# A decoder layer on one core: the mask's score bound moved into self-attention's tail, weight splits moved to a step's begin, first queries ahead of the values

## What is computed

```
x = layernorm(x + self_attention(x))          # 32 heads of 16, causal, biases on q, k, v and out
x = layernorm(x + cross_attention(x, ctx))    # 32 query heads, 8 key/value heads of 128, rotary angles, mask
x = layernorm(x + experts(x))                 # 16 experts of 256, 4 of them per token, and a shared one

# cross-attention, the part that the change touches:
scores = einsum('bhgqd,bhkd->bhgqk', qg, k) / sqrt(128)
masked = where(mask.astype(bool), scores, -1e9)
w = softmax(masked, axis=-1)
```

## Time and profile before

| | |
|---|---|
| median of 3 runs | 1770.8 us (1770.31 to 1776.01) |
| the profiled execution's own time | 1773.97 us |
| its span, first to last instruction | 1772.2 us |
| granted TensorE clock, mean | 0.982 of full |
| PE / DVE / ACT / POOL busy | 96 / 72 / 52 / 54 % |
| self-attention | 0 to 303 us |
| cross-attention | 303 to about 1300 us |
| experts | behind that |

### The profile page before, as it was taken

The page is one execution under the profiler, slowest core; times in us unless marked ns, Lnnn a source line. Parts: engine busy times, 40 slices in busy tenths (PEclk is TensorE's granted clock), DMA queues, the critical chain, the costliest instruction groups (busy, mean ns, idle before and its releaser), DMA issues. The chain is left out here.

```text
span 1772.2 us, 39039 instructions
## 1 busy us (share of the span) xinstructions
PE 1695.6 (96%) x15461; PEld 968.1 (55%) x15461; DVE 1267.5 (72%) x2048; ACT 919.0 (52%) x1518; POOL 964.8 (54%) x875
## 2 busy tenths in 40 slices
PE   6899998699999999999999999999889999999997
PEld 4666665365555555555555555555555555455553
DVE  5777776678888888888888888888786444344445
ACT  5776764555546564646464555455742333333334
POOL 5556672745645454646464646464743555455545
PEclk9999999899999999999999999999988999999999
DMA  4522312311312222214131222121166778887658
GB/s 147 146 65 47 85 48 36 117 37 58 110 62 83 83 68 89 97 42 149 37 108 61 72 72 96 37 104 40 61 226 198 153 151 222 221 208 153 115 100 300
DMA packets 88897, 190.68 MB, mean 108 GB/s; under 512 B 14800, under 2 KB 33744, under 8 KB 86672
## 3 DMA queue, kind: packets, MB, share of 16 engines
q1 hardware_dynamic: 65232, 130.72, 22.1%
q0 software_dynamic: 22912, 57.32, 15.8%
q10 hardware_dynamic: 576, 0.14, 0.0%
HBM read 124.95 MB, written 63.21 MB: 106 GB/s over the span
## 5 line engine op out<-in xcount | busy, mean ns | idle before, releaser
L1112 POOL TENSOR_TENSOR xa_sc<-xa_sc,xa_rs 128x1024 f32<-128x1024 f32 x32 | 60.9, 1903 | 374.4 <-DVE xa_rs L1360 374.4
L1099 POOL TENSOR_TENSOR xa_xs<-xa_xs,sn 128x512 f32<-128x512 f32 x160 | 234.1, 1463 | 45.7 <-ACT xa_xs L1153 45.7
L288 PE MATMUL bank<-xhl,front_h 128*128 128x512 f16 x640 | 245.4, 383 | 10.9 <-DVE front_l L648 9.7
L289 PE MATMUL bank<-xhl,front_h 128*128 128x512 f16 x640 | 245.2, 383 | 0.0
L290 PE MATMUL bank<-xhl,front_l 128*128 128x512 f16 x640 | 245.0, 383 | 0.0
L1104 POOL TENSOR_TENSOR xa_rr<-xa_x,xa_xs 128x512 f32<-128x512 f32 x160 | 232.9, 1456 | 12.7 <-DVE xa_x L1260 0.2
L2006 POOL DMA_INDIRECT scratch_y<-raw_front,moe_to x79 | 125.3, 1586 | 149.1 <-DVE mo_zl L2060 126.8
L288 PE MATMUL bank<-out_h,xa_oh 128*128 128x512 f16 x512 | 194.1, 379 | 10.3 <-DVE xa_ol L1242 6.7
L290 PE MATMUL bank<-out_h,xa_ol 128*128 128x512 f16 x512 | 194.0, 379 | 0.0
L289 PE MATMUL bank<-out_l,xa_oh 128*128 128x512 f16 x512 | 194.0, 379 | 0.0
L1152 ACT ACTIVATE xa_xs<-bank 64x512 f32<-64x512 f32 x160 | 95.1, 595 | 140.7 <-PE bank L290 126.5
(11 more groups left out here) (318 smaller groups left out, 4665.5 us busy)
## 6 DMA issues: line engine op xcount, KB each, us to landing
xa_rawc<-in_ew SPq DMA_DIRECT2D x32, 768.0 KB, 5.5
moe_ring<-scratch_w SPq DMA_DIRECT2D x16, 1536.0 KB
scratch_w<-xa_chunk_h SPq DMA_DIRECT2D x32, 384.0 KB, 2.3
scratch_w<-xa_chunk_l SPq DMA_DIRECT2D x32, 384.0 KB, 3.3
raw_front<-in_xwq SPq DMA_DIRECT2D x8, 1024.0 KB, 7.8
raw_out<-in_xwo SPq DMA_DIRECT2D x8, 1024.0 KB, 5.3
scratch_y<-acc SPq DMA_DIRECT2D x6, 1024.0 KB, 5.8
acc<-in_x POOLq DMA_DIRECT2D x4, 1024.0 KB, 7.7
```

The source lines that it names most:

```text
L288: pe.matmul(out_ap, ah, bh, start=start and m == 0, stop=False)
L289: pe.matmul(out_ap, ah, bl, start=False, stop=False)
L1099: PO.mark(pool.tensor_tensor(xr, xr, sn[:, :].rearrange("p (a s) -> p a s", a=1) .to_broadcast([P, QT // S, S]), ALU.mult), f"sm{r}", st)
L1112: PO.mark(pool.tensor_tensor(s4, s4, rs[:, :, :].rearrange("p h (t a) -> p (h t) a", a=1) .to_broadcast([P, 16, S]), ALU.mult), "nm", st)
```

## The change

1. `bound` becomes a buffer that lives through both attentions. Its bytes (128 partitions by 2048 f32) serve self-attention as `late_h` (split weights of groups 2 and 3, high part) and `kk` (keys), which had buffers of their own.
2. At self-attention's end SP waits for the last projection "q" and the last masked keys "ko", then loads the mask into `bound`. POOL turns it into the bound behind its last step. Load and computation are gone from cross-attention, and the wait of DVE for them.
3. The splits of groups 2 and 3 and of self-attention's output weight move on ACT to the begin of steps 1, 2 and 3. On DVE they stay where they were.
4. In step 0 of self-attention the queries are loaded, split and projected ahead of the values. ACT copies the queries between its two masked keys and the values last.
5. In the tail PE transposes only the first quarter of the last probabilities, then makes `next_keys`, then the other three quarters, two of the three tiles of `next_values`, `back_pv`, and the third tile. DVE makes "ol" behind the fourth "sb".
6. The output weight of cross-attention's group 0 is split in step 0, not 1: on ACT between the first and the second rotation's copies, on DVE in four pieces of 512 columns.

```diff
@@ self_attention, buffers
-                late_h, late_l = b("late_h", [P, 2 * GW], F16), b("late_l", [P, 2 * GW], F16)
+                shared = bound[:, :, :].rearrange("p b k -> p (b k)").bitcast(F16)
+                late_h, late_l = shared[:, 0:2 * GW], b("late_l", [P, 2 * GW], F16)
-                kk, kx = b("kk", [P, 2, QT], F16), b("kx", [P, 2, 2, QT], F16)
+                kk, kx = shared[:, 2 * GW:2 * GW + 2 * QT].rearrange("p (a t) -> p a t", a=2), b("kx", [P, 2, 2, QT], F16)
@@ sync
-                    for n, w in ((0, wkT), (2, wvT), (1, wqT)):
+                    for n, w in enumerate((wkT, wqT, wvT)):
...
+                    last = step_of(STEPS - 1)
+                    sp.wait_ge(PE.sem, PE.value("q", last))
+                    sp.wait_ge(AC.sem, AC.value("ko", last))
+                    for h in range(2):
+                        sp.dma_start(bound[64 * h:64 * h + 64, :, :], maskf.rearrange("b q k -> q b k")).then_inc(s_mask, 16)
@@ gpsimd, behind the 16 steps
+                    pool.wait_ge(s_mask, 32)
+                    limit = bound[:, :, :].rearrange("p b k -> p (b k)")
+                    chain(pool.tensor_scalar(limit, limit, 0.0, 0.0, ALU.is_equal, ALU.is_equal))
+                    chain(pool.tensor_scalar(limit, limit, BIG, -1e9 * float(HD2) ** 0.5, ALU.mult, ALU.add))
@@ scalar, step(n)
+                        if n in (1, 2):
+                            front_high(n + 1)
+                        if n == 3:
+                            act.wait_ge(s_ro, 16)
+                            act.activation(out_h[:, :], raw_out[:, :], ACT.Copy, scale=WS).then_inc(s_wo_a, 1)
                         if n > 1:
                             back_o(st, n - 2)
...
                         else:
                             front_high(1)
-                        keys_of(st, 0)
-                        keys_of(st, 1)
-                        if n in (1, 2):
-                            front_high(n + 1)
-                        if n == 3:
-                            act.wait_ge(s_ro, 16)
-                            act.activation(out_h[:, :], raw_out[:, :], ACT.Copy, scale=WS).then_inc(s_wo_a, 1)
+                            keys_of(st, 0)
+                            act.wait_ge(s_first_q, 1)
+                            queries_of(st)
+                            keys_of(st, 1).then_inc(s_first_qh, 1)
+                            values_out(st)
@@ tensor, tail
-                    back_p(done, (0, 1))
-                    back_p(done, (2, 3))
+                    back_p(done, (0,))
                     pe.wait_ge(s_cq, 2)
                     pe.wait_ge(s_upper, 1)
                     pe.wait_ge(DV.sem, DV.value("sb2", done))
                     next_keys(pe)
+                    back_p(done, (1,))
+                    back_p(done, (2, 3))
+                    pe.wait_ge(DV.sem, DV.value("sb3", done))
+                    next_values(pe, (0, 1))
                     back_pv(done)
-                    pe.wait_ge(DV.sem, DV.value("sb3", done))
-                    next_values(pe)
+                    next_values(pe, (2,))
@@ cross_attention, gpsimd
-                            if first and (q, r) == (0, 2):
-                                mask_bound(pool)
@@ cross_attention, scalar
                         copies(st, 0)
-                        copies(st, 1)
-                        if q == 1:
+                        if alone:
+                            act.wait_ge(s_ro, 16)
+                            act.activation(wo_h[:, :, :], raw_o[:, :, :], ACT.Copy, scale=WS).then_inc(s_first_out, 1)
+                        copies(st, 1, ("woh",) if first and q == 1 else ())
+                        if q == 1 and i:
@@ cross_attention, vector
+                    def out_lo(dve, h):
+                        dve.scalar_tensor_tensor(wo_l[:, h, :], raw_o[:, h, :], WS, wo_h[:, h, :], ALU.mult, ALU.subtract)
...
-                        if q == 1:
+                        if q == 1 and i:
                             dve.wait_ge(AC.sem, AC.value("woh", st))
```

More of the change, by code:

```diff
@@ L349, in self_attention @@
                 s_acc = [sem(f"sa_rows{n}") for n in range(NQ)]
-                s_pre_a, s_pre_v, s_zero, s_mask, s_bias = (sem("sa_" + n) for n in ("pre_a", "pre_v", "zero", "mask", "s_bias"))
+                s_pre_a, s_pre_v, s_zero, s_causal, s_bias = (sem("sa_" + n) for n in ("pre_a", "pre_v", "zero", "mask", "s_bias"))
+                s_first_q, s_first_qh = sem("sa_first_q"), sem("sa_first_qh")
                 s_wo_a, s_wo_v = sem("sa_out_h"), sem("sa_out_l")
@@ L533, in _ @@
                         act.activation(xh[:, 2 * h:2 * h + 2, 0:QT], first_in[:, 2 * h:2 * h + 2, :], ACT.Copy).then_inc(s_q0h, 1)
-                    for n in (0, 2, 1):
+                    for n in range(3):
                         act.wait_ge(s_w0[n], 16)
@@ L644, in _ @@
                             dve.tensor_scalar(bias[:, :, :], rawb[:, :, :], WS, None, ALU.mult).then_inc(s_bias, 1)
-                    for m, n in enumerate((0, 2, 1)):
-                        dve.wait_ge(s_pre_a, m + 1)
+                    for n in range(3):
+                        dve.wait_ge(s_pre_a, n + 1)
                         c = slice(n * P, (n + 1) * P)
@@ L720, in soft @@
                             below_most(st, j)
+                        if n == STEPS:
+                            back_out_lo(st, n - 2)
                         for j in range(2):
@@ L782, in _, with projected @@
                     pe.wait_ge(s_pre_v, 1)
+                    def projected(name, st, n):
+                        tok, c = slice(st.i * QT, (st.i + 1) * QT), slice(n * P, (n + 1) * P)
+                        return three_pass(pe, home[name][:, :], [(wf_h[st.q][:, k, c], wf_l[st.q][:, k, c], xh[:, k, tok],
+                                                                  xl[:, k, tok]) for k in range(KD)])
                     def feature_major(name, st, n, before=(), after=()):
-                        tok, c = slice(st.i * QT, (st.i + 1) * QT), slice(n * P, (n + 1) * P)
                         names = (*before, name, *after)
-                        PE.mark(three_pass(pe, home[name][:, :], [(wf_h[st.q][:, k, c], wf_l[st.q][:, k, c], xh[:, k, tok],
-                                                                   xl[:, k, tok]) for k in range(KD)]), names[0], st, names[1:])
+                        PE.mark(projected(name, st, n), names[0], st, names[1:])
                     def values(st, also=()):
@@ L875, in step @@
                             pe.wait_ge(s_pre_v, 2)
-                        values(st, () if n else ("pt2", "pt3"))
+                            projected("q", st, 1).then_inc(s_first_q, 1)
+                            pe.wait_ge(s_pre_v, 3)
+                        values(st, () if n else ("pt2", "pt3", "q", "tu", "pv0", "pv1", "w"))
                         if n:
@@ L1020, in _ @@
                     sp.sem_inc(s_cw, 32)
-                    for h in range(2):
-                        sp.dma_start(bound[64 * h:64 * h + 64, :, :], maskf.rearrange("b q k -> q b k")).then_inc(s_mask, 16)
                     sp.wait_ge(s_zero, 1)
@@ L1299, in step @@
                             chunk_lo().then_inc(s_first_l, 1)
-                        rotated_lo(st, 0)
-                        if q == 1:
+                        rotated_lo(st, 0, ("wol",) if first and q == 1 else ())
+                        if q == 1 and i:
                             dve.wait_ge(AC.sem, AC.value("woh", st))
@@ L1307, in step @@
                         cosine(st, 2, ("pl0", "pl1") if alone else ())
+                        if alone:
+                            dve.wait_ge(s_first_out, 1)
+                            out_lo(dve, 0)
                         if not alone:
@@ L1313, in step @@
                         cosine(st, 3)
+                        if alone:
+                            out_lo(dve, 1)
                         rotated_lo(st, 2)
@@ L1322, in step @@
                         rotated_lo(st, 3, ("lo2", "lo3") if alone else ())
+                        if alone:
+                            out_lo(dve, 3)
                         if i == NG - 1 and q >= 2:
@@ L2338, in build @@
             ch, cl = sb("ch", [P, KD, T], F16, held), sb("cl", [P, KD, T], F16, held)
+            bound = sb("bound", [P, B, S], F32, held)
             cs, sn = sb("cs", [P, S], F32, held), sb("sn", [P, S], F32, held)
@@ L2369, in first_keys, with first_values @@
                                                           for k in range(KD)]), "r0", Step(0, 0))
-            def first_values(pe):
+            def first_values(pe, ts):
                 wh, wl = (blocks(z, KD)((GQ + 2) * HD2) for z in (front_h, front_l))
                 c = (GQ + 1) * HD2
-                for t in range(TQ - 1):
+                for t in ts:
                     tk = slice(t * P, (t + 1) * P)
```

66 lines of the change are left out of this document (34 added, 32 removed).

## The result

The changed kernel takes 1755.3 us in the median of its runs (1754.52 to 1757.31), the kernel before 1770.55 beside it: a ratio of 0.9907, 95% interval 0.9894 to 0.992. It is 15.25 us faster. A second set on another chip gives 1755.83 against 1772.34, 0.9913 (0.9899 to 0.9926). Forecast was 1744.9, a gain of 25.9. The direction holds and the time lies in the range (1738 to 1757), near its upper end; the size is 10.6 off. The pair of profiled executions differs by more, 1773.97 against 1755.72.

A forecast was written before the change was run, and what follows sets the result against it. The prediction took PE, busy 96% of the span, to bound the kernel. Its terms 11.7 + 1.6 + 0.7 + 11.9 = 25.9 us, taken from the median 1770.8, gave 1744.9, range 1738 to 1757.

The forecast's parts named there:

- The splits: Self-attention steps 1 to 3: ACT's weight splits at the step's begin remove three waits ahead of the scores; gain 11.7 us.
- 8.5 + 4.2 − 1.0: Self-attention's splits: 8.5 us of PE idle removed, 4.2 from the clock's return, less 1.0 of leftover waits.
- First queries: Self-attention step 0: queries ahead of values cut the first scores' wait from 1.75 to 0.1 us; gain 1.6.
- The tail: Self-attention's end: `next_keys` fills two waits for exponentials, 1.8 us together, leaving 0.3 and 0.8; gain 0.7.
- Rival E: Self-attention's end: POOL's mask work holds up the block, costing the time POOL ends after 302 us; slower, 2%.
- Cross-attention: Cross-attention steps 0 and 1: moving the mask and splitting the output weight earlier gain 7.7 + 2.9 + 1.3 = 11.9 us.
- two stand on the path ..., and I have counted them at 0.8: Cross-attention step 0: two, or four, of DVE's output weight pieces stand on the path to the second scores, costing 0.8 us.
- rival C: Cross-attention step 0: four output weight pieces collide with POOL's rotations, second scores' chain 4.3 us longer, total 1749.2; 14%.
- 2.9 + 1.3: Cross-attention step 1: the wait for the probabilities' low part ends 2.9 us earlier, and a half-clock stretch goes for 1.3.
- B: Self-attention steps 1 to 3: splits ahead of the exponentials delay the transposes and the clock still falls; loss 9.1 us, 1754; 12%.
- D: Cross-attention's begin: the clock recovers better, with no stretch at 0.50; 3 us more gain, 1742; 7%.
- F: Self-attention: the scores in effect follow "vbh" and the waits stay; only the other parts count, 14.2 us, 1756.6; 3%.

The follow-up runs named there:

- no_pieces: The changed kernel with cross-attention's output weight split in step 1 by one instruction of 2048 columns, not in quarters in step 0; ratio 0.9900 to the kernel before.
- firstq_alone: The kernel before with only the first step's queries put ahead of its values; median 0.9 us faster, interval −0.7 to 2.5.
- tail_alone: The kernel before with only self-attention's tail in the new order; 1.6 us slower by the ratio, with an interval that ends at no change.
- xa_alone: The kernel before with the mask's bound made in self-attention's tail and the output weight split in quarters in step 0; gain 10.3 us by profile.
- mask_alone: The kernel before with the mask's bound made in self-attention's tail, output weight split in step 1 as before; gain 8.7 us by profile.
- after_again: The changed kernel as it is, run and profiled a second time; 1755.83 us against 1772.34 for the kernel before, ratio 0.9913.
- shift184: The changed kernel with 92 tiny matmuls (184 instructions) ahead of PE's first; by the medians as fast as the changed kernel.
- warm256: The changed kernel with 128 tiny matmuls (256 instructions) ahead of PE's first; first scores at 20.25 us instead of 19.84, nothing won.
- bias_later: The changed kernel with the output bias's 1 MB accumulating transfer one step later; no median given, stall at 2753 3.80 us instead of 1.09.
- pieces_later: The changed kernel with the second to fourth piece of the output weight's low part moved later on DVE; median 1754.95 us.
- both_moved: The changed kernel with the output weight's later pieces moved later on DVE and the bias transfer 5 us earlier; 1749.56 us, 6.3 below the changed kernel.

## Why the prediction was right in direction and too large

*The splits, 11.7: too large by 3.8.* The mechanism held: "ql" had waited for ACT's and DVE's splits, all three waits went, and in this profile the clock stayed up. The step that failed is "8.5 + 4.2 − 1.0". It took a wait that ends for an idle that ends. The supply of PE's instructions needed 3.2 of the same us: the kernel with the splits alone shows the amount, and the shifted list shows the cause. The clock with its leftovers came to 2.6 for 3.2. I read that the scores of step 4 start with no wait, and did not read the row 2.4 us behind it, 1.19 under "issue", in a step without a split. The scores of step 4 came at 79.3, not near 75.

*First queries, 1.6:* 1.64 in the kernel with this part alone. That the number is so near is partly luck: the wait left is 0.52 and not 0.1, and the clock's phase made up for it.

*The tail, 0.7: it gave 0.3.* Both leftovers I named are there (0.49 and 0.77), with a third of 0.16. In the changed kernel's own profile the slow stretch behind it takes more than this back. The mask cost nothing, as said: it ended at 279.5, before the block's end at 295. Rival E had no part.

*Cross-attention, 11.9: it gave 9.3.* The mask's share was nearly as sized: 9.1 at the second scores with no pieces and no slow stretch ahead of them. The forecast was 7.7 + 0.8, or 10.0 without the 1.5 charged for such a stretch. The step that failed is "two stand on the path ..., and I have counted them at 0.8": the quarters cost 1.8 at the first scores and, with the clock, 3.0 at the second, so rival C (4.3) came in part. One of the four pieces was held itself (1.25 for 0.68), and the low parts of the queries behind them took 1.61 to 1.75 where no_pieces has 0.95 to 1.21. Behind step 0 the quarters gave 3.5 for 2.9 + 1.3. The new wait of 1.50 for `xa_ol` takes a part of that back: with the long wait for `xa_ptl` gone, PE comes to these matmuls before DVE is through with the low parts of their input. No run took this wait away. The prediction also read POOL's first mask operation as one of 1.90 that DVE had stretched; it takes 7.11 in the tail too. The sum did not rest on this.

*From the sum to the median.* By profiles the four parts make 7.9 + 1.6 + 0.3 + 9.3 = 19.1, and the pair of profiles 18.3. The medians make 15.3. The profiled execution of before stood 3.4 above its median and had a mean clock of 0.982. Of 22 runs of before on one chip, the seven with 0.980 to 0.982 took 1772.05 to 1775.9, the fifteen with 0.984 and more 1770.57 to 1774.03. So it had more time at the lower clock than a typical run, and I subtracted a gain read in it from a median with less. Where a typical run has less of it, no run shows. It need not be behind the three waits: the four other profiles that keep them (firstq_alone, tail_alone, xa_alone, mask_alone) have 10.2 to 13.7 us at 0.50 between 37 and 79, and that of before has 10.2. Which stretches make up the 3.0 between the pair of profiles and the medians stays open.

*The rivals.* B did not come: ahead of the transposes the only waits for `sa_sc` were 0.2 in step 0's successor and 0.8 in the tail. D did not: 10.2 us at 0.50 remain between 309 and 331 (17.1 before), 6.8 in the second profile. F did not: the three waits went.

## What to carry over

Before a wait is costed as a gain, look for what else comes true only at its end: here the next piece of the instruction list arrived during it. Count the instructions of an engine between two long ones; where some 250 small matmuls and loads run in under 3 us, the fetch is the next bound, and a large transfer issued just before makes it worse. A short operation put into an engine's gap is free only if it ends before the gap does in the company it has there, not alone. Take clock gains from more than one execution.

## What the runs showed of the hardware

- PE's instructions arrive in packets of 16 KB, one for each 256 records of its list (128 for 32,749, 129 for 33,005). With the DMA engines free, the packet for the next border was issued 0.5 to 1.0 us after a border was passed; it took about 1.0, and PE went on 1.2 to 1.5 after its end. That makes about 3.1 us per 256, an estimate from the table. Behind a transfer that keeps the DMA engines busy the packet came 3 to 7 us behind the border (5.80 at 1985 in the changed kernel, 7.01 in after_again).
- Beside POOL, a DVE instruction with two SBUF inputs ended 0.55 after POOL's own, five times in cross-attention's step 0. Timelines of DVE and of POOL, changed kernel:

```profile
303.98 1.61 DVE L1290 TENSOR_TENSOR xa_rql<-xa_rr,xa_rqh 128x512 f16<-128x512 f32 x1
307.41 1.25 DVE L1294 SCALAR_TENSOR_TENSOR out_l<-raw_out,out_h 128x512 f16<-128x512 f32 x1
308.59 1.74 DVE L1290 TENSOR_TENSOR xa_rql<-xa_rr,xa_rqh 128x512 f16<-128x512 f32 x1
...
303.24 1.80 POOL L1123 TENSOR_TENSOR xa_xs<-xa_xs,sn 128x512 f32<-128x512 f32 x1
306.85 1.26 POOL L1123 TENSOR_TENSOR xa_xs<-xa_xs,sn 128x512 f32<-128x512 f32 x1
308.19 1.59 POOL L1128 TENSOR_TENSOR xa_rr<-xa_x,xa_xs 128x512 f32<-128x512 f32 x1
```

  303.98 + 1.61 is 305.59 and POOL's end 305.04; 308.66 stands to 308.11 and 310.33 to 309.78 alike. Alone the same instruction takes 0.68. It goes the other way too: POOL's 1.80 at 303.24, issued just behind a DVE piece at 303.23, is 1.27 when nothing stands in its way. The Trainium skill's page "SBUF — State Buffer", in "Who interferes with whom", says that such a pair shares ports under an exclusive lock, so that the one issued first holds off the other; these rows agree, also in size. The 4.88 of the earlier trace rows does not: DVE, issued 0.2 after POOL's 7.11, ended 2.0 before it and not behind it. No run here shows why.
- POOL's comparison with zero over 128x2048 took 7.11 in both kernels, in one beside DVE's 4.88, in the other with DVE at other work, and so in five more profiles with it in the tail: the time is its own. The multiply and add of the same size took 1.90.
- TensorE's clock differs between runs of one kernel at the same place. The stretch near 282 is in four profiles of kernels with the mask in the tail (the changed one, xa_alone, shift184, warm256), not in six others with it (mask_alone, no_pieces, bias_later, pieces_later, both_moved, after_again), and in none of the four without. Whether POOL's work there makes it likelier stays open.
